# Attention with exact row maxima on one core: the maxima's matmuls move to 48-row operands in the two row halves of TensorE, in batches of four heads

## The chip, the cores and the metric

One core of a Trainium2 chip runs the whole kernel. The metric is the device time of one execution in microseconds (us). A comparison is made with runs of the kernel before on the same chip.

## What is computed

x is 2 x 2048 x 256. Sixteen heads of 16 channels attend causally, in float32, then comes an output projection, a residual with layer norm, a product of int8-quantised rows with int8-quantised weights, and a second residual with layer norm.

```python
Q, K, V = (proj(Wq), proj(Wk), proj(Wv))                 # x @ W.T, split into 16 heads of 16
scores = scale * einsum('bhtd,bhsd->bhts', Q, Kb)        # keys in the future: -inf
m_new = maximum(m, max(scores, -1)); p = exp(scores - m_new)
l = corr * l + sum(p);  acc = corr * acc + p @ Vb        # corr = exp(m - m_new)
x = layernorm(x + (acc / l) @ Wo.T)
x = layernorm(x + int8_rows(x) @ int8_columns(rhs))      # times the scales of rows and columns
```

## The kernel before

The 32 pairs of batch and head are worked in 8 groups of 4 heads (HG = 4). Queries come in 4 chunks of 512 columns (CHUNKS, CH), keys in blocks of 128. A step (STEPS) is one chunk of queries against one block of keys, for the four heads of a group; a group has 40 steps, of which the last four of each chunk lie on the diagonal and are only 512, 384, 256 and 128 columns wide.

The front (0 to 127 us) projects Q and K and splits each value into three bf16 parts, whose sum is the float32 value. The parts are stored in DRAM (qparts, kparts) and come back as stacks: QS and KS hold 96 rows, six products of parts (Q_TERMS, K_TERMS), 16 channels each. Three more rows of QS hold the row's maximum, negated and split in three, against three rows of ones in KS, so that one matmul over 99 rows gives score minus maximum.

So each score is computed twice. First the maxima: an item (ITEMS) is one tile of 128 queries against up to 512 keys for two heads. Its two matmuls (L683, 96 rows, each followed on the diagonal by a mask matmul, L686) fill one of the two slots of ps_max, two banks each, and VectorE reduces the slot to block_max (L956). A group has 80 items, 32 of them on the diagonal (8 of each width 512, 384, 256 and 128). combine folds them per chunk, a transposition (turn_maxima, L694), ScalarE (L891) and GpSimd (split_maxima, L1186 to L1193) make the three rows, and SyncE writes them into QS (load_max_rows). Then the scores: one matmul a head and step (L728) into one of the three banks of ps_score, ScalarE takes the exponential (L908), GpSimd cuts the diagonal, and two steps later the values' matmuls (L709, float32, four heads side by side in four groups of 32 columns of the array) add it to ps_acc. ScalarE copies ps_acc per chunk (copy_acc, L896), SyncE stores it (store_heads).

The order on TensorE is written out by a planner at build time: quota walks the steps with costs in columns and says after which score matmul which item comes (QUOTA). The 46 first items (AHEAD) of a group are made during the group before, those of group 0 in the front (FRONT_QUOTA). Groups 0 to 5 are of kind "steady" (80 items each), group 6 is "full" (114, since it also makes all that is left for group 7), group 7 is "last" (none; the end of the kernel, per half chunk, is woven into it). Groups 1 to 4 run in a hardware loop of two turns of two groups; the others are straight-line code.

QS and KS exist twice (p = group modulo 2): while one group is worked, SyncE's queue loads the other's (next_stacks, 12 DMAs a chunk, L407), between the stores of heads and the rows of maxima.

Of the kernel before, what the change touches and what calls it, by code (L numbers as in the profile page):

```python
# [39 lines left out]
K_TERMS = [0, 0, 0, 1, 1, 2]  # L40
MIX_FROM = 12
# [27 lines left out]
def build(nc, x, wq, wk, wv, wo, ffn, out):  # L69
# [9 lines left out]
    KROWS = STACK + PARTS  # L79
    assert (B, D, DH, HALVES) == (2, 256, 16, 2) and T % (2 * CH) == 0  # L80
# [13 lines left out]
    assert NI % MAX_SLOTS == 0  # L94
# [15 lines left out]
    FORM, LOAD, READ, READ_FROM = 576, 256, 2.5, 340  # L110

    def quota(stream):
# [3 lines left out]
        made = lambda m: PAIR * (max(ITEM_COLS[m] // PAIR, LOAD) + (P if ITEMS[m][1] == ITEMS[m][0] // TPC else 0))  # L116
        read = lambda m: READ_FROM + READ * ITEM_COLS[m]

        def place(pace, early):
            at, done, free, seen, n, out = 0, 0, [0] * MAX_SLOTS, 0, 0, []  # L120
            for k, (c, kb) in enumerate(STEPS):
                out.append([])
                for j in range(HG):
                    at += max(CH - skip(c, kb), LOAD)
                    if n < len(stream) and free[n % MAX_SLOTS] <= at + early and seen * pace <= at:
                        at = max(at, free[n % MAX_SLOTS]) + made(stream[n][1])
                        done = max(done, at) + read(stream[n][1])
                        free[n % MAX_SLOTS] = done
                        seen += read(stream[n][1])
                        n += 1  # L130
# [102 lines left out]
    with ExitStack() as ctx:  # L233
# [20 lines left out]

        QS_words = sb("QS", [P, 2 * HG * T // 2], F32)
        QS = QS_words[:, :].bitcast(BF16).rearrange("p (s c j n) -> p s c j n", s=2, c=CHUNKS, j=HG)
        KS = sb("KS", [KROWS, 2, CHUNKS, HG, CH], BF16)
# [52 lines left out]
        room = [(end_words[:, :], 6), (V_words, 8), (QS_words[:, 0:HG * T // 2], 4)]  # L310
# [52 lines left out]
        s_qs = [[sem(f"q_stack{p}_in{c}") for c in range(CHUNKS)] for p in range(2)]  # L363
        s_ks = [[sem(f"k_stack{p}_in{c}") for c in range(CHUNKS)] for p in range(2)]
# [15 lines left out]
        SL = 16 * len(Q_TERMS)  # L380
        OST = 16 * (HG + 1)
# [19 lines left out]
        with nc.Block() as block:  # L401
            @block.sync
            def _(sp):
                def load_stack(q, p, c, stack, src, terms, done):

                    for t, a in enumerate(terms):
                        sp.dma_start(stack[DH * t:DH * t + DH, p, c, :, :],  # L407
                                     src[a, bass.ds((2 * q + p) * GR, GR), c * CH:c * CH + CH]
                                     .rearrange("(j d) n -> d j n", d=DH)).then_inc(done, 16)

                def load_stacks(q, p, c):
                    load_stack(q, p, c, QS, qparts, Q_TERMS, s_qs[p][c])
                    load_stack(q, p, c, KS, kparts, K_TERMS, s_ks[p][c])

                def load_max_rows(g, p, c):
                    wait_apart(sp, s_ms, splits(g, c), sp_mark)
                    for a in range(PARTS):
                        sp.dma_start(QS[STACK + a:STACK + a + 1, p, c].rearrange("a j (r n) -> a (j r) n", r=TPC),
                                     max_parts[:, c, a, :]).then_inc(s_mrow[c], 16)
# [9 lines left out]
                def group(q, p):  # L429
                    g, kind = 2 * q + p, KIND(2 * q + p)  # L430
                    first = isinstance(g, int) and g == 0
                    nq, np_ = (q, 1) if p == 0 else (q + 1, 0)

                    def next_stacks(c):
                        if not first:
                            load_stacks(nq, np_, c)

                    if not first:
                        wait_apart(sp, s_st, score_base(g), sp_mark)
                    next_stacks(0)  # L440
# [37 lines left out]
                for n in range(XCHUNKS):  # L478
                    if n + 2 < XCHUNKS:
                        load_x(n + 2)  # L480
                    if n == FRONT_TURN + 1:
                        for c in EARLY:
                            load_max_rows(0, 0, c)
                    store_parts(n)
                    if n < CHUNKS:
                        sp.wait_ge(stored[n % 2], 16 * QK_UNITS * (n // 2 + 1))
                        load_stacks(0, 0, n)
                    else:
                        load_stacks(0, 1, n - CHUNKS)
# [9 lines left out]
                def load(m):  # L499
# [3 lines left out]
                    if m == SLOTS - 2:  # L503
                        sp.wait_ge(s_st, score_base(GROUPS - 1))
# [29 lines left out]
                with sp.Fori(0, GROUPS // 2 - 2) as h:  # L534
# [16 lines left out]
                for c in LATE:  # L551
                    load_max_rows(GROUPS - 1, 1, c)
# [21 lines left out]
            def _(pe):  # L574
# [69 lines left out]
                def front():  # L644
# [7 lines left out]
                    for n in range(XCHUNKS):  # L652
                        for u in range(UNITS_X):
# [10 lines left out]
                            for m in range(done, FRONT_QUOTA[n][u]):  # L664
# [3 lines left out]
                                item(0, 0, m)  # L668
# [4 lines left out]
                def item(q, p, n):  # L673

                    i, b, w, h = ITEMS[n]
                    if n in FIRST_ITEM:
                        pe.wait_ge(s_qs[p][i // TPC], SL * (q + 1))
                        pe.wait_ge(s_ks[p][i // TPC], SL * (q + 1))
                    at_least(pe, s_reduced, item_use(2 * q + p, n) - MAX_SLOTS + 1)
                    diag = b == i // TPC  # L680
                    for t in range(PAIR):
                        bank, j = ps_max[:, n % MAX_SLOTS * PAIR + t, :], h * PAIR + t
                        m = pe.matmul(bank[:, 0:w], QS[0:STACK, p, i // TPC, j, i % TPC * P:i % TPC * P + P],  # L683
# [608 lines left out]
```

## Time and profile before

| | |
|---|---|
| median of 3 runs | 1066.67 us (1065.55 to 1070.85) |
| the profiled execution | 1070.6 us, span 1068.8 us |
| PE busy | 1000.2 us, 94% |
| DVE busy | 828.0 us, 77% |
| ACT busy | 707.8 us, 66% |
| POOL busy | 264.4 us, 25% |
| DMA moved | 66.39 MB, 62 GB/s |

PE is TensorE's matmuls, PEld its weight loads, DVE VectorE, ACT ScalarE, POOL GpSimd, SPq SyncE's queue. A matmul's duration contains its way through the array, and consecutive ones overlap; what counts is the distance from one start to the next. The copies of ps_acc at L896 mark the stages: each group has four, at fixed steps, so the distance between the same copy of two groups is the length of a group.

### The profile page before, as it was taken

How to read it: one execution, taken by the hardware profiler on the slowest of the kernel's cores; microseconds unless marked ns; L12 is line 12 of the kernel's file. 1: busy time of each engine (PE TensorE's matmuls, PEld its weight loads, DVE VectorE, ACT ScalarE, POOL GpSimd, SP SyncE). 2: the span in 40 equal slices, each digit the busy share in tenths (PEclk: the TensorE clock that was granted, in tenths of full speed). 3: DMA queues.
4: the chain of work that ended last, by engine and by line, in shares of the span. 5: the costliest groups of instructions: out<-in, count | busy, mean ns of one | idle time of the engine just before them, and what ended most of it. 6: DMA issues, size and time to landing. Idle time of an engine off the chain costs nothing.

```text
span 1068.8 us, 20004 instructions
## 1 busy us (share of the span) xinstructions
PE 1000.2 (94%) x6280; PEld 396.8 (37%) x6280; DVE 828.0 (77%) x1083; ACT 707.8 (66%) x1471; POOL 264.4 (25%) x435
## 2 busy tenths in 40 slices
PE   8999999999999999899999999999999899998972
PEld 5555433333333333233333333333333222443431
DVE  5466677777878777678777777877888888599897
ACT  3444467777777778577777777777766466787730
POOL 3534520112111211120112011201111101565644
PEclk9999989999999999999999999999999999999995
DMA  5657500002011201120102010301120420315501
GB/s 167 188 170 229 162 10 7 7 22 81 7 38 31 72 7 37 29 61 21 37 11 80 17 37 18 85 7 36 35 72 7 115 44 1 101 50 154 152 30 50
DMA packets 71786, 66.39 MB, mean 62 GB/s; under 512 B 15112, under 2 KB 65608, under 8 KB 71684
## 3 DMA queue, kind: packets, MB, share of 16 engines
q1 hardware_dynamic: 71684, 65.10, 21.8%
q8 instruction: 56, 0.92, 0.4%
q14 instruction: 46, 0.38, 0.1%
HBM read 43.25 MB, written 21.35 MB: 60 GB/s over the span
## 4 chain that ended last, share of the span: by engine, by line
PE 82%; DVE 7%; ACT 3%; DMA 3%; issue 2%; POOL 1%; SPq 1%; ACTq 0%; POOLq 0%; DVEq 0%
PE ps_acc L709 24%; PE ps_score L728 22%; PE ps_max L683 21%; PE ps_score L602 5%; DVE block_max L956 4%; PE ps_score L609 3%; ACT PR L908 2%; PE ps_max L686 2%; PE ps_max L783 1%; DMA end_slots<-heads_out 1%; PE ps_acc L583 1%; DMA V<-heads_out 1%; DMA row_sums<-accS 1%; ACT accS L896 1%; PE ps_score L694 1%
## 5 line engine op out<-in xcount | busy, mean ns | idle before, releaser
L956 DVE TENSOR_REDUCE block_max<-ps_max 128x2 f32<-128x1024 f32 (+3 forms) x640 | 658.1, 1062 | 191.5 <-PE ps_max L683 95.0
L908 ACT ACTIVATE PR<-ps_score 128x512 f32<-128x512 f32 (+3 forms) x1280 | 618.9, 536 | 225.3 <-PE ps_score L728 210.0
L728 PE MATMUL ps_score<-QS,KS 99*128 99x512 bf16 (+3 forms) x1280 | 392.9, 354 | 20.2 <-ACT PR L908 12.7
L683 PE MATMUL ps_max<-KS,QS 96*128 96x512 bf16 (+3 forms) x1280 | 359.3, 351 | 15.2 <-DVE block_max L956 12.1
L709 PE MATMUL ps_acc<-PR,VG 128*32 128x512 f32 (+3 forms) x2560 | 303.3, 546 | 0.1
L728 PEld LDWEIGHTS ps_score<-QS,KS 99*128 99x128 bf16 x1280 | 118.9, 97 | 339.3 <-ACT PR L908 233.4
L683 PEld LDWEIGHTS ps_max<-KS,QS 96*128 96x128 bf16 x1280 | 120.5, 98 | 106.3 <-DVE block_max L956 42.0
L1178 POOL TENSOR_SCALAR_AFFINE_SELECT PR<-PR 128x512 f32<-128x512 f32 x128 | 81.7, 638 | 314.7 <-ACT PR L908 314.5
L686 PE MATMUL ps_max<-mask_q,ident_b 128*128 128x128 bf16 x512 | 102.6, 220 | 0.0
L709 PEld LDWEIGHTS ps_acc<-PR,VG 128*32 128x32 f32 x2560 | 50.7, 108 | 96.6 <-ACT PR L908 54.9
L1186 POOL CAST max_parts<-neg_max 16x128 bf16<-16x128 f32 (+1 forms) x31 | 8.8, 285 | 275.7 <-ACT neg_max L891 272.5
L602 PE MATMUL ps_score<-PR,wT 128*128 128x512 f32 x128 | 60.4, 598 | 0.8 <-ACT neg_max L870 0.7
L686 PEld LDWEIGHTS ps_max<-mask_q,ident_b 128*128 128x128 bf16 x512 | 50.6, 99 | 22.7 <-issue 2.8
L1165 POOL TENSOR_TENSOR end_slots<-PR,end_slots 128x512 bf16<-128x512 f32 x32 | 37.0, 1157 | 65.0 <-ACT end_slots L857 65.0
L852 ACT CAST end_slots<-ps_score 128x512 bf16<-128x512 f32 x32 | 18.8, 586 | 45.8 <-PE ps_score L602 45.8
L602 PEld LDWEIGHTS ps_score<-PR,wT 128*128 128x128 f32 x128 | 23.5, 192 | 21.0 <-issue 18.2
L609 PE MATMUL ps_score<-wT,PR 128*128 128x256 f32 x128 | 31.3, 391 | 0.0
L1170 POOL COPY VG<-V 128x256 f32<-128x256 f32 (+1 forms) x32 | 12.6, 394 | 71.7 <-PE ps_acc L709 71.3
L1005 DVE TENSOR_TENSOR PR<-ps_score,end_slots 128x512 f32<-128x512 f32 x32 | 21.8, 684 | 8.0 <-ACT end_slots L852 7.0
L609 PEld LDWEIGHTS ps_score<-wT,PR 128*128 128x128 f32 x128 | 24.4, 194 | 4.4
L896 ACT COPY accS<-ps_acc 128x512 f32<-128x512 f32 x32 | 19.1, 597 | 7.7 <-PE ps_acc L709 7.6
L1221 POOL TENSOR_TENSOR rstd<-var_eps,minus_half 128x2 f32<-128x2 f32 x32 | 23.5, 734 | 2.7
(122 smaller groups left out, 465.3 us busy)
## 6 DMA issues: line engine op xcount, KB each, us to landing
QS<-qparts SPq DMA_DIRECT2D x192, 64.0 KB, 2.3
KS<-kparts SPq DMA_DIRECT2D x192, 64.0 KB, 2.3
qparts<-end_slots SPq DMA_DIRECT2D x16, 384.0 KB, 5.3
kparts<-end_slots SPq DMA_DIRECT2D x16, 384.0 KB, 4.5
PR<-in_L_attn_x SPq DMA_DIRECT2D x8, 512.0 KB, 4.4
heads_out<-accS SPq DMA_DIRECT2D x124, 32.0 KB
end_slots<-in_L_attn_x SPq DMA_DIRECT2D x4, 512.0 KB, 9.8
out_y<-end_slots SPq DMA_DIRECT2D x8, 256.0 KB, 2.1
```

The source lines that it names most:

```text
L602: m = pe.matmul(bank, wT[:, w, mh, nh * P:nh * P + P], xT[:, n % 2, mh, :], start=mh == 0, stop=mh == HALVES - 1)
L609: m = pe.matmul(bank[:, t * D:t * D + D], xT[:, n % 2, mh, tile * P:tile * P + P], wT[:, 2, mh, :], start=mh == 0, stop=mh == HALVES - 1)
L683: m = pe.matmul(bank[:, 0:w], QS[0:STACK, p, i // TPC, j, i % TPC * P:i % TPC * P + P], KS[0:STACK, p, b, j, 0:w], start=True, stop=not diag)
L686: m = pe.matmul(bank[:, w - P:w], ident_b[:, :], mask_q[:, :], start=False, stop=True)
L709: m = pe.matmul(ps_acc[EYE * j:EYE * j + EYE, s:CH], VG[:, kb, j, :], PR[:, k % 4, j, 0:CH - s], start=kb == 0, stop=k == LAST[c])
L728: pe.matmul(bank[:, 0:CH - s], KS[:, p, kb // TPC, j, kb % TPC * P:kb % TPC * P + P], QS[0:KROWS, p, c, j, s:CH], start=True, stop=True).t ...
L896: act.copy(accS[:, c % 2, :], ps_acc[:, :]).then_inc(s_accS, 1)
L908: act.activation(PR[:, k % 4, j, 0:w], ps_score[:, score_slot(pos), 0:w], ACT.Exp, scale=SCALE).then_inc(s_exp, 1)
L956: dve.tensor_reduce(block_max[:, h * PAIR:h * PAIR + PAIR, i, b], ps_max[:, slot_at:slot_at + PAIR, 0:w], AX.X, ALU.max).then_inc(s_reduce ...
L1165: pool.tensor_tensor(parts[:, n % 2, u, 2, :], rest[:, q % RESTS, :], parts[:, n % 2, u, 1, :], ALU.subtract).then_inc(part3, 1)
L1178: pool.affine_select(out=block, in_=block, compare_op=ALU.is_ge, fill=0.0, base=0, pattern=[[0, HG], [1, P]], channel_multiplier=-1).then_ ...
L1221: pool.tensor_tensor(rstd[:, z, which, rows], var_eps[:, z, which, rows], minus_half[:, :], ALU.pow)\
```

## The change

1. Maxima's operands. New tensors QM and KM hold 48 rows (MROWS: three products of parts, MAX_TERMS) for a head in rows 0 to 47 and for a second head in rows 64 to 111 (ROW_HALF), two halves a group, two groups. They replace the 96-row stacks for the maxima (the maximum is thus computed from fewer parts; scores minus maxima still use all six products). The two matmuls of an item now read the two row halves and write two banks.
2. Items come in batches of two (four heads). On the diagonal the mask matmuls of the whole batch come first, and wait until both slots are free; the 48-row matmuls are then added on top. The planner prices a pair as one matmul and a batch with SEEN = 480 columns more.
3. QS and KS exist once. A chunk of QS is loaded for the next group when this group's last step of that chunk has been scored, a chunk of KS when the last chunk of queries has passed it. The operands of maxima for the next group are loaded at the group's start, 12 DMAs of 128 KB.
4. The loop over groups 1 to 4 is written out on every engine.
5. The ones of KS are set in 4 memsets, not 8; the end's buffers lie in QM and KM.

In the front, items are still made one by one.

```diff
+MAX_TERMS = [(0, 0), (1, 0), (0, 1)]
+ROW_HALF = 64
-    FORM, LOAD, READ, READ_FROM = 576, 256, 2.5, 340
+    FORM, LOAD, READ, READ_FROM, SEEN = 576, 256, 2.5, 340, 480
-        made = lambda m: PAIR * (max(ITEM_COLS[m] // PAIR, LOAD) + (P if ITEMS[m][1] == ITEMS[m][0] // TPC else 0))
+        made = lambda m: max(ITEM_COLS[m] // PAIR, LOAD) + (PAIR * P if ITEMS[m][1] == ITEMS[m][0] // TPC else 0)
+        later = lambda m: SEEN + made(m) if ITEMS[m][1] < ITEMS[m][0] // TPC else 0
...
-                    if n < len(stream) and free[n % MAX_SLOTS] <= at + early and seen * pace <= at:
-                        at = max(at, free[n % MAX_SLOTS]) + made(stream[n][1])
-                        done = max(done, at) + read(stream[n][1])
+                    if n < len(stream) and seen * pace <= at and max(free[0], free[1] - later(stream[n][1])) <= at + early:
+                        at += SEEN
+                        for m in stream[n:n + MAX_SLOTS]:
+                            at = max(at, free[n % MAX_SLOTS]) + made(m[1])
+                            done = max(done, at + SEEN) + read(m[1])
...
+                def load_max_operands(g, p, done, t0=0, t1=T):
+                    for r in range(PAIR):
+                        for t, (a, b) in enumerate(MAX_TERMS):
+                            at = ROW_HALF * r + DH * t
+                            for rows, src in ((QM[at:at + DH, p, :, t0:t1], qparts[a]), (KM[at:at + DH, p, :, t0:t1], kparts[b])):
+                                sp.dma_start(rows, src[bass.ds(g * GR, GR), t0:t1]
+                                             .rearrange("(h r d) t -> r d h t", r=PAIR, d=DH)[r]).then_inc(done, 16)
...
                     if not first:
                         store_heads(g - 1, CHUNKS - 1)
-                    load_max_rows(g, p, 2)
+                    load_max_rows(g, 2)
+                    if not first:
+                        wait_apart(sp, s_reduced, NI * g, sp_mark)
+                        load_max_operands(g + 1, 1 - p, s_am[1 - p])
+                    next_q(0)
                     store_heads(g, 0)
-                    next_stacks(1)
-                    next_stacks(2)
+                    next_q(1)
                     store_heads(g, 1)
-                    load_max_rows(g, p, 3)
-                    load_max_rows(g + 1, np_, 0)
+                    load_max_rows(g, 3)
+                    load_max_rows(g + 1, 0)
...
-                    next_stacks(3)
+                    next_q(2)
                     store_heads(g, 2)
-                    load_max_rows(g + 1, np_, 1)
+                    next_k(0)
+                    load_max_rows(g + 1, 1)
+                    for c in range(1, CHUNKS):
+                        next_k(c)
+                    next_q(3)
...
+                def items(q, p, some):
+                    for n in some:
+                        i, b, w, h = ITEMS[n]
+                        if b == i // TPC:
+                            at_least(pe, s_reduced, item_use(2 * q + p, n) - MAX_SLOTS + 1)
+                            for t in range(PAIR):
+                                pe.matmul(ps_max[:, n % MAX_SLOTS * PAIR + t, w - P:w], ident_b[:, :], mask_q[:, :],
+                                          start=True, stop=True)
+                    for n in some:
...
+                        if b != i // TPC:
+                            at_least(pe, s_reduced, item_use(2 * q + p, n) - MAX_SLOTS + 1)
+                        for t in range(PAIR):
+                            r = ROW_HALF * t
+                            m = pe.matmul(ps_max[:, n % MAX_SLOTS * PAIR + t, 0:w], QM[r:r + MROWS, p, h, i * P:i * P + P],
+                                          KM[r:r + MROWS, p, h, b * CH:b * CH + w], start=b != i // TPC, stop=True,
+                                          skip_group_check=b == i // TPC)
+                        m.then_inc(s_piece, 1)
...
-                pe.wait_ge(s_set, 1 + 2 * CHUNKS)
+                pe.wait_ge(s_set, 1 + CHUNKS)
...
-                with pe.Fori(0, GROUPS // 2 - 2) as h:
+                for h in range(GROUPS // 2 - 2):
                     group(h, 1)
                     group(h + 1, 0)
```

## Rows read from the trace of the kernel before

**Rows 1.** The page: the chain that ended last, shares of the span by engine.

```profile
PE 82%; DVE 7%; ACT 3%; DMA 3%; issue 2%; POOL 1%; SPq 1%; ACTq 0%; POOLq 0%; DVEq 0%
```

**Rows 2.** Busy time by stretch: start:end, length, PE, PEld, DVE, ACT, POOL, clock.

```profile
555.00:660.00 105.00, 104.07 (x710) 37.52 (x708) 82.46 (x85) 79.27 (x168) 16.88 (x36) 1.00 0.13 37
```

**Rows 3.** Timeline, last copy of ps_acc of groups 0, 1, 2, 4, 5, 6: start, duration (us).

```profile
240.14 0.59 ACT L896 COPY accS<-ps_acc 128x512 f32<-128x512 f32 x1
...
345.67 0.59 ACT L896 COPY accS<-ps_acc 128x512 f32<-128x512 f32 x1
...
457.67 0.59 ACT L896 COPY accS<-ps_acc 128x512 f32<-128x512 f32 x1
...
668.75 0.59 ACT L896 COPY accS<-ps_acc 128x512 f32<-128x512 f32 x1
...
773.68 0.59 ACT L896 COPY accS<-ps_acc 128x512 f32<-128x512 f32 x1
...
910.27 0.66 ACT L896 COPY accS<-ps_acc 128x512 f32<-128x512 f32 x1
```

**Rows 4.** Timeline of one steady step: values, score, item, three scores, item, values.

```profile
600.65 0.39 PE L728 MATMUL ps_score<-QS,KS 99*128 99x512 bf16 x1
600.66 0.32 PEld L683 LDWEIGHTS ps_max<-KS,QS 96*128 96x128 bf16 x2
600.87 0.60 PE L683 MATMUL ps_max<-KS,QS 96*128 96x512 bf16 x2
601.31 0.89 PE L728 MATMUL ps_score<-QS,KS 99*128 99x512 bf16 x3
601.51 2.38 DVE L956 TENSOR_REDUCE block_max<-ps_max 128x2 f32<-128x1024 f32 x2 [0.53 <-PE ps_max L683]
602.03 0.60 PE L683 MATMUL ps_max<-KS,QS 96*128 96x512 bf16 x2
602.56 1.06 PE L709 MATMUL ps_acc<-PR,VG 128*32 128x512 f32 x8
603.55 0.10 PEld L728 LDWEIGHTS ps_score<-QS,KS 99*128 99x128 bf16 x1 [0.84 <-ACT PR L908]
```

**Rows 5.** Timeline, values' matmuls of 128 columns between two scores.

```profile
239.44 0.43 PE L709 MATMUL ps_acc<-PR,VG 128*32 128x128 f32 x8
239.79 0.80 PE L728 MATMUL ps_score<-QS,KS 99*128 99x256 bf16 x3
```

**Rows 6.** Groups by shape: busy us, mean ns.

```profile
L956 DVE TENSOR_REDUCE block_max<-ps_max 128x2 f32<-128x768 f32 x64 | 59.9, 957 | 28.9 <-PE ps_max L686 28.3
L956 DVE TENSOR_REDUCE block_max<-ps_max 128x2 f32<-128x512 f32 x64 | 42.6, 688 | 12.2 <-PE ps_max L686 11.9
L956 DVE TENSOR_REDUCE block_max<-ps_max 128x2 f32<-128x256 f32 x64 | 26.3, 423 | 22.4 <-PE ps_max L686 22.0
```

**Rows 7.** Timeline where the loop turns back: TensorE's first instruction, SyncE's DMAs.

```profile
450.14 0.61 PE L728 MATMUL ps_score<-QS,KS 99*128 99x512 bf16 x1 [3.40 <-issue]
450.18 3.73 SPq L407 DMA_DIRECT2D KS<-kparts  x6
```

**Rows 8.** Timeline in group 6: VectorE, and an item that waits for it.

```profile
861.12 3.49 DVE L956 TENSOR_REDUCE block_max<-ps_max 128x2 f32<-128x1024 f32 x3 [0.46 <-PE ps_max L683]
862.40 0.61 PE L683 MATMUL ps_max<-KS,QS 96*128 96x512 bf16 x2 [0.45 <-DVE block_max L956]
```

**Rows 9.** Timeline of the front and of its end.

```profile
108.66 0.60 PE L683 MATMUL ps_max<-KS,QS 96*128 96x512 bf16 x2
109.10 1.89 PE L609 MATMUL ps_score<-wT,PR 128*128 128x256 f32 x8
...
125.21 0.59 ACT L864 COPY V<-ps_score 128x512 f32<-128x512 f32 x1 [1.06 <-PE ps_score L609]
127.30 0.39 PE L728 MATMUL ps_score<-QS,KS 99*128 99x512 bf16 x1 [1.69 <-POOL KS L1258]
131.69 1.89 PE L728 MATMUL ps_score<-QS,KS 99*128 99x384 bf16 x5
```

More of the change, by code:

```diff
@@ L667, in front @@
                                     pe.wait_ge(f_copied, 2)
-                                item(0, 0, m)
+                                items(0, 0, [m])
                             done = FRONT_QUOTA[n][u]
@@ L671, in front @@
                             turn_first_maxima()
[L673 to L683, printed above, removed]
-                                      KS[0:STACK, p, b, j, 0:w], start=True, stop=not diag)
-                        if diag:
-                            m = pe.matmul(bank[:, w - P:w], ident_b[:, :], mask_q[:, :], start=False, stop=True)
-                    m.then_inc(s_piece, 1)
+                def items(q, p, some):
[7 more added lines that the diff above has]
+                    for n in some:
+                        i, b, w, h = ITEMS[n]
+                        if n in FIRST_ITEM and isinstance(q, int) and (q, p) == (0, 0):
+                            pe.wait_ge(s_first[i // TPC], AM)
+                        elif n == 0:
+                            pe.wait_ge(s_am[p], AM * (q + p))
+                        if b != i // TPC:
[6 more added lines that the diff above has]
+                        m.then_inc(s_piece, 1)
@@ L727, in group @@
                             bank = ps_score[:, score_slot(pos), :]
-                            pe.matmul(bank[:, 0:CH - s], KS[:, p, kb // TPC, j, kb % TPC * P:kb % TPC * P + P],
-                                      QS[0:KROWS, p, c, j, s:CH], start=True, stop=True).then_inc(s_st, 1)
-                            while n < QUOTA[kind][k][j]:
-                                on, m = STREAM[kind][n]
-                                item(*groups[on], m)
-                                n += 1
+                            pe.matmul(bank[:, 0:CH - s], KS[:, kb // TPC, j, kb % TPC * P:kb % TPC * P + P],
+                                      QS[:, c, j, s:CH], start=True, stop=True).then_inc(s_st, 1)
+                            if n < QUOTA[kind][k][j]:
+                                on = STREAM[kind][n][0]
+                                some = [m for o, m in STREAM[kind][n:QUOTA[kind][k][j]] if o == on]
+                                items(*groups[on], some)
+                                n += len(some)
                             if kind == "last" and j % 2:
@@ L821, in _ @@
                 group(0, 0)
-                with pe.Fori(0, GROUPS // 2 - 2) as h:
+                for h in range(GROUPS // 2 - 2):
                     group(h, 1)
@@ L934, in _ @@
                 group(0, 0)
-                with act.Fori(0, GROUPS // 2 - 2) as h:
+                for h in range(GROUPS // 2 - 2):
                     group(h, 1)
@@ L1061, in _ @@
                 group(0, 0)
-                with dve.Fori(0, GROUPS // 2 - 2) as h:
+                for h in range(GROUPS // 2 - 2):
                     group(h, 1)
@@ L1263, in _ @@
                 group(0, 0)
-                with pool.Fori(0, GROUPS // 2 - 2) as h:
+                for h in range(GROUPS // 2 - 2):
                     group(h, 1)
```

74 lines of the change are left out of this document (39 added, 35 removed).

## The prediction, made before the changed kernel ran

> **What bounds the kernel now.** I read the page's chain of waits first [rows 1]: the chain that ended last is 82% TensorE. Then the stages: the last copy of ps_acc of each group [rows 3] gives 105.53 us for group 1 (345.67 - 240.14), 112.00 for group 2 (457.67 - 345.67), twice 105.54 for groups 3 and 4 (668.75 - 457.67) and 104.93 for group 5. Group 6, which reads 114 items, takes 910.27 - 773.68 = 136.6. The busy time by stretch comes next: in a steady group of 105 us [rows 2] TensorE is busy 104, VectorE 82, ScalarE 79, GpSimd 17: TensorE is the bound there, with VectorE 20% behind. The timeline of one step [rows 4] says what the 105 us are made of: a matmul of 512 columns starts 0.22 us after the one before it (two of an item take 0.44), and its weights are loaded while the one before it streams, so a load costs nothing. In group 6 it is VectorE: three reads without a gap in 3.49 us, and an item that waits 0.45 us for them [rows 8].
>
> **Part 1, the pairs (gain).** Two heads in two row halves should stream in the time of one. Of the 80 items of a group 56 are 512 wide, and 8 each 384, 256 and 128. A pair saves 0.22 us at 512 [rows 4] and, in proportion to the columns, 0.165 and 0.11; at 128 I take nothing. 56 x 0.22 + 8 x 0.165 + 8 x 0.11 = 14.5 us a group. No row shows row halves at work. The nearest is the values: four heads in four column groups, float32, 8 instructions of 512 columns, done in 1.00 us [rows 4]; with 128 columns in 0.35 [rows 5]. That is 0.65 us for 384 columns more, 1.7 ns a column for all four heads, four cycles at 2.4 GHz: the four heads run at once at full rate. So I take full overlap; the lower bound is none (rival C).
>
> **Part 2, going into the halves and out (cost).** The same rows show what it costs to change how the array is cut. The last item before the values starts at 602.03 and streams until 602.47; the values start at 602.56, 0.09 later. Their slope puts 512 columns at 0.86 us, and the next score's weights start 0.99 us and the score 1.00 us after them, so 0.14 to come back; at 128 columns 0.35 - 0.22 = 0.13. The score's weights are loaded only at 603.55, when the values are through: on this border a load isn't hidden. Together 0.25 us there and back, taking the entry as 0.10. I call the same cost for a batch X. Its bounds: 0 (the row cut needs no emptying of the array, as between two matmuls of equal cut) and 0.35 (going in loads weights of 128 columns, not of 32, for two halves; a recorded load is 0.10 us, unhidden). I take 0.25, the row nearest to it. Worked through by its own rule, the planner places every item of a steady group in pairs: 40 batches, 10.0 us a group.
>
> The Trainium skill, page "TensorEngine Tiling (Array Packing)", section "Key Properties", says that changing the tiling mode drains TensorE, which speaks against this change; the gaps around the values agree with it, and no row shows whether it holds for rows as for columns. By that sentence X isn't 0. The page "TensorE: Matmul & The Clock Gate", Part 3, has weight loads overlap running matmuls only in another row group; the second pair of a batch would then pay its load, 0.10 us more. The load under a running matmul of the same rows [rows 4] speaks against it for the whole array, and none shows it for the halves.
>
> **Part 3, waiting for both slots.** Before, an item needs one free slot while VectorE reads the other, which hides TensorE's work. A batch off the diagonal keeps this: its first pair goes into slot 0 while slot 1 is read. A batch on the diagonal (16 of 40) starts its masks only when both are free. VectorE starts 0.42 us after the second matmul of an item starts (601.51 against 601.09), and a batch of two full items keeps it 2.38 us [rows 4]. So a batch that begins at b has both slots free at about b + 0.1 + 0.42 + 2.38 = b + 2.9. The next comes a step later: 4 scores 0.88, batch 0.44 + 0.25, values with their border 1.10 = 2.67. On the diagonal it waits 0.25 us if it directly follows a full batch, less or nothing if the plan put it later, as it often does. 16 x 0.15 = 2.5 us a group; bounds 0 and 16 x 0.35 = 5.6. Behind the waiting instruction in TensorE's queue stand the scores, for which ScalarE waits: it has some 25 us of slack a group [rows 2].
>
> A steady group: -14.5 + 10.0 + 2.5 = -2.0 us. Six of them (0 to 5): -12.
>
> **Part 4, group 6.** VectorE bounds it. Its 114 reads are 84 of 1.19 us [rows 4] and 10 each of 0.96, 0.69 and 0.42 [rows 6]: 121 us, the group 136.6. Halving TensorE's work there frees nothing. New is that VectorE idles in each of 21 diagonal batches from the end of its last read to the first pair: 4 masks of 128 columns 0.22, entry 0.1, 0.42 until it may read, with the masks' wait together 0.8 us, or 16 us; and the plan puts its last batch at step 35, with some 5.5 us of scores behind it. 121 + 16 + 5.5 = 142.5, +6 us. Bounds: 0 (its idle time in group 6 before is as long, and may be replaced) and +12 (0.15 us at each other batch too).
>
> **Part 5, the front.** Items are still single there, and TensorE is back to back: an item of 512 takes 0.44 us between two projections [rows 9]. 46 borders at 0.25 = 11.5 us, against 28 full items x 0.22 + 6 x 0.165 + 6 x 0.11 = 7.8 saved: +3.7.
>
> **Part 6, the start of group 0.** TensorE waits 1.69 us for the memset of ones, while the copy it needs too ended at 125.80 [rows 9]. With four memsets fewer it starts some 1.4 us earlier. After that gap five scores of 384 take 1.89 us [rows 9], half speed: the clock fell to 1.2 GHz. If it doesn't, up to 5 us more; I take 2. Sum -3.4 (0 to -6.4).
>
> **Part 7, the loop.** Where it turns back, TensorE waits 3.40 us for nothing the profile shows [rows 7] and then runs at half clock for a while; group 2 is 6.4 us longer than group 1 [rows 3]. There is one such turn. Straight-line groups (5, 6) show no such stop, so the longer program should cost nothing: -6.4 (0 if a fetch of instructions takes its place).
>
> **Part 8, SyncE's queue and single stacks: nothing.** Stacks still cost 48 DMAs a group, plus 12 of the new operands; six issue in 3.7 us [rows 7], so 7.5 us more of some 50. The tightest new wait is K's chunk 0: released at step 27, needed 13 steps later, some 34 us, against 4 us of issue and the landing. Behind it stand the next group's rows of maxima for chunk 1, which are turned only at step 31. Q's and K's chunk 3 come at step 39 and are needed at step 24 of the next group. If one did come late, TensorE would stop at the head of a chunk; none has less than 10 us in hand.
>
> **The sum,** against the profiled execution's 1070.6 us: -12 + 6 + 3.7 - 3.4 - 6.4 = -12.1, or 1058.5. Written with X open: 987 + 286 X. The median of the runs shown is 3.9 us under the profiled one, so 1054.6; I say **1054 us**, 1.2% faster.
>
> **The rivals.**
> A, the border of the halves is cheap, X from 0 to 0.2. For it: only column cuts are seen to cost. At 0.15 the sum gives 1030, as a median 1026.
> B, slower: the border costs more than the values' one, since each way in must load 128 columns of weights unhidden for both halves. X = 0.35: 1087, as a median 1083. It decides from X = 0.29, where the sum equals the time before; the place is each of the 286 batches. For it: the score's load at 603.55 waits for the values' end. Against: 0.14 us for the way back already has such a load in it. The rule on loads named above is this rival by another mechanism: +0.10 a batch, the same 0.35.
> C, the halves don't run at once: no pair saves. 987 + 94.8 + 71.5 = 1153, as a median 1149. Against it the values' four heads at once.
> D, VectorE becomes the bound in steady groups. Its 82 us plus 16 x 0.8 plus 24 x 0.27 (the second batch's read begins 0.25 us after the first's end) is 101; with every misplaced batch added, groups stay at 105, and the sum is 1070.6 + 6 + 3.7 - 9.8 = 1070.5, as a median 1067.
>
> **Chances.** Forecast 0.45, A 0.22, B 0.16, D 0.12, C 0.05. Low end: A down to X = 0.13, 1020. High end: B at 1084. What lies outside is C and the tails of A and B, some 2 in 10. Half a per cent, 1061 to 1072, is about what a measurement here can tell: faster 0.60 (A and most of the forecast), same 0.16 (D and the edge of the forecast), slower 0.24 (B, C, the upper edge).
>
> **What would show it.** The distance between equal copies of ps_acc: 103.5 us in groups 1 to 5 with none at 112, 142 in group 6. In a full step the distance from the score before a batch to the score after it: 0.22 + 0.69. The two matmuls of a pair start within 0.1 us of each other and the next pair 0.22 later; if 0.44, C. VectorE's gap before a diagonal batch 0.8 us. No TensorE wait on a DMA. The prediction is wrong first of all through X, at 2.9 us for each 0.01 of it.

## The result, and the profile after

The changed kernel takes 1072.9 us (median of 20 runs, 1067.0 to 1079.0), the kernel before in the same runs 1065.9. The ratio is 1.0061, 95% interval 1.0043 to 1.0079: slower by 0.6%, where 1054 and 1.2% faster were forecast. The time lies inside the stated range (1020 to 1084), on the other side of no change.

The page of the changed kernel, in the rows that moved: busy time and share, the slices, the chain.

```profile
PE 968.6 (90%) x6280; PEld 325.9 (30%) x6280; DVE 816.7 (76%) x1083; ACT 693.2 (65%) x1471; POOL 256.7 (24%) x431
PE   8999999999999999999999999999887888998862
PEclk9999999999999999999999999999999789999995
PE 63%; DVE 23%; ACT 7%; DMA 3%; issue 2%; SPq 1%; POOL 1%; POOLq 0%; DVEq 0%; ACTq 0%
```

TensorE is busy 32 us less than before, and the span is 1.6 us longer. In the chain that ended last VectorE has gone from 7% to 23% and ScalarE from 3% to 7% [rows 1]: TensorE now waits for others. The slices of group 6 (the 29th to the 34th) have lost their nines, and two of them (0.7 and 0.8) show a lower granted clock.

The last copy of ps_acc of groups 0, 1, 2, 5 and 6 in the changed kernel, as in [rows 3]:

```profile
236.09 0.58 ACT L931 COPY accS<-ps_acc 128x512 f32<-128x512 f32 x1
...
341.04 0.58 ACT L931 COPY accS<-ps_acc 128x512 f32<-128x512 f32 x1
...
445.99 0.58 ACT L931 COPY accS<-ps_acc 128x512 f32<-128x512 f32 x1
...
761.37 0.61 ACT L931 COPY accS<-ps_acc 128x512 f32<-128x512 f32 x1
...
911.53 0.66 ACT L931 COPY accS<-ps_acc 128x512 f32<-128x512 f32 x1
```

Distances between such copies, here and for the experiments below (us; the end of group 0 is the copy's own time). The distances are those of one profiled execution each, the medians those of 20 runs (changed), 4 to 10 (e1, e2, e5, e7, e9, e10), 2 (e3, e4, e8) or 1 (e6, e11):

| kernel | end of 0 | a steady group | group 6 | median |
|---|---|---|---|---|
| before | 240.1 | 105.5, one of 112.0 | 136.6 | 1065.9 |
| changed | 236.1 | 104.95 | 150.2 | 1072.9 |
| e1, before, loop written out | 233.5 | 104.7 | 137.4 | 1058.8 |
| e2, diagonal batches in turn | 236.3 | 105.5 | 133.6 | 1058.2 |
| e3, reads halved | 230.2 | 100.2 | 119.0 | 1010.3 |
| e4, exponentials halved | 233.1 | 102.3 | 149.5 | 1053.4 |
| e5, in turn in group 6 only | 237.0 | 104.95 | 134.1 | 1056.4 |
| e6, e3 and e4 together | 227.0 | 97.4 | 115.7 | 989.3 |
| e7, batch in mid step | 237.5 | 105.4, two longer | 135.2 | 1061.0 |
| e8, single items | 236.5 | 104.6 | 131.2 | 1051.7 |
| e9, the same again | 234.6 | 104.6 | 132.4 | 1051.0 |
| e10, single items at two places | 234.7 | 102.3 | 133.0 | 1039.2 |
| e11, both heads in one half | 256.4 | 118.3 | 155.6 | 1163.8 |

So groups 1, 3 and 4 gained 0.6 us each at first sight (group 5, at 105.5, lost as much), the turn of the loop is gone, and group 6 gave 13.6 us back. One step of a steady group, TensorE alone, is the counterpart of [rows 4]:

```profile
628.23 0.38 PE L762 MATMUL ps_score<-QS,KS 99*128 99x512 bf16 x1
628.54 0.61 PE L718 MATMUL ps_max<-KM,QM 48*128 48x512 bf16 x4
629.08 0.82 PE L762 MATMUL ps_score<-QS,KS 99*128 99x512 bf16 x3
629.83 1.06 PE L743 MATMUL ps_acc<-PR,VG 128*32 128x512 f32 x8
630.83 0.61 PE L762 MATMUL ps_score<-QS,KS 99*128 99x512 bf16 x2
```

The batch of four matmuls takes 0.54 us from its start to the next score: 2 x 0.216 for two pairs, 0.11 to come out. It starts 0.31 after the score, 0.22 of streaming and 0.10 to go in. So the halves do run at once, and a border costs 0.21 us (in and out together), not 0.25. That much of the mechanism works: this step takes 2.60 us, where one of before takes 2.91 (603.56 - 600.65, the second from the score at 603.56 that follows the row at 603.55 in [rows 4]). The gain is lost elsewhere. Here is the start of a diagonal batch in group 6:

```profile
802.52 0.38 PE L762 MATMUL ps_score<-QS,KS 99*128 99x512 bf16 x1
802.52 0.32 PEld L706 LDWEIGHTS ps_max<-mask_q,ident_b 128*128 128x128 bf16 x2
802.74 0.28 PE L706 MATMUL ps_max<-mask_q,ident_b 128*128 128x128 bf16 x2
...
803.34 0.28 PE L706 MATMUL ps_max<-mask_q,ident_b 128*128 128x128 bf16 x2 [0.33 <-DVE block_max L991]
803.56 0.61 PE L718 MATMUL ps_max<-KM,QM 48*128 48x512 bf16 x4
803.99 2.36 DVE L991 TENSOR_REDUCE block_max<-ps_max 128x2 f32<-128x1024 f32 x2 [0.71 <-PE ps_max L718]
```

TensorE sets the masks of the first slot, stands until VectorE has freed the second, and VectorE then stands 0.71 us until the first pair is there. Both engines idle in turn.

### The profile page after: what moved, and what is told of

It reads as the page before. It is cut to its first block, busy times and chain, and to the rows that moved or that the text cites. A ratio compares the mean times of both kernels' runs of the same rounds, so it can differ in the third digit from the quotient of the medians.

```text
span 1070.4 us, 17302 instructions
## 1 busy us (share of the span) xinstructions
PE 968.6 (90%) x6280; PEld 325.9 (30%) x6280; DVE 816.7 (76%) x1083; ACT 693.2 (65%) x1471; POOL 256.7 (24%) x431
## 4 chain that ended last, share of the span: by engine, by line
PE 63%; DVE 23%; ACT 7%; DMA 3%; issue 2%; SPq 1%; POOL 1%; POOLq 0%; DVEq 0%; ACTq 0%
DVE block_max L991 19%; PE ps_acc L743 19%; PE ps_score L762 18%; PE ps_max L718 12%; ACT PR L943 6%; PE ps_score L628 5%; PE ps_max L706 3%; PE ps_score L635 2%; PE ps_max L818 2%; DMA end_slots<-heads_out 1%; ACT accS L931 1%; PE ps_acc L609 1%; DMA kparts<-end_slots 1%; DVE stats L1105 1%; DMA row_sums<-accS 1%
## 5 line engine op out<-in xcount | busy, mean ns | idle before, releaser
L991 DVE TENSOR_REDUCE block_max<-ps_max 128x2 f32<-128x1024 f32 (+3 forms) x640 | 649.2, 1061 | 194.5 <-PE ps_max L718 192.8
L943 ACT ACTIVATE PR<-ps_score 128x512 f32<-128x512 f32 (+3 forms) x1280 | 604.9, 537 | 253.2 <-PE ps_score L762 250.4
L762 PE MATMUL ps_score<-QS,KS 99*128 99x512 bf16 (+3 forms) x1280 | 361.7, 356 | 28.4 <-ACT PR L943 24.5
L718 PE MATMUL ps_max<-KM,QM 48*128 48x512 bf16 (+3 forms) x1280 | 198.3, 357 | 29.3 <-DVE block_max L991 22.9
L762 PEld LDWEIGHTS ps_score<-QS,KS 99*128 99x128 bf16 x1280 | 97.7, 97 | 380.8 <-ACT PR L943 289.3
L718 PEld LDWEIGHTS ps_max<-KM,QM 48*128 48x128 bf16 x1280 | 49.1, 94 | 133.3 <-DVE block_max L991 86.4
L706 PE MATMUL ps_max<-mask_q,ident_b 128*128 128x128 bf16 x512 | 56.7, 223 | 8.5 <-DVE block_max L991 7.9
L706 PEld LDWEIGHTS ps_max<-mask_q,ident_b 128*128 128x128 bf16 x512 | 40.5, 99 | 34.0 <-DVE block_max L991 13.3
L1205 POOL COPY VG<-V 128x256 f32<-128x256 f32 x32 | 12.7, 396 | 158.1 <-PE ps_acc L743 157.9
```

What stands on the lines that cost most here:

```text
L706: pe.matmul(ps_max[:, n % MAX_SLOTS * PAIR + t, w - P:w], ident_b[:, :], mask_q[:, :], start=True, stop=True)
L718: m = pe.matmul(ps_max[:, n % MAX_SLOTS * PAIR + t, 0:w], QM[r:r + MROWS, p, h, i * P:i * P + P], KM[r:r + MROWS, p, h, b * CH:b * CH + w] ...
L762: pe.matmul(bank[:, 0:CH - s], KS[:, kb // TPC, j, kb % TPC * P:kb % TPC * P + P], QS[:, c, j, s:CH], start=True, stop=True).then_inc(s_st, 1)
L943: act.activation(PR[:, k % 4, j, 0:w], ps_score[:, score_slot(pos), 0:w], ACT.Exp, scale=SCALE).then_inc(s_exp, 1)
L991: dve.tensor_reduce(block_max[:, h * PAIR:h * PAIR + PAIR, i, b], ps_max[:, slot_at:slot_at + PAIR, 0:w], AX.X, ALU.max).then_inc(s_reduce ...
```

## The experiments

Two theories were set against each other first. Theory 1: the loss is in slots, above all the wait for both before a diagonal batch. Theory 2: four heads in one batch keep ScalarE and the score banks waiting.

**e1.** The kernel before, with the loop alone written out:

```diff
-                with pe.Fori(0, GROUPS // 2 - 2) as h:
+                for h in range(GROUPS // 2 - 2):
```

> The kernel before with nothing changed but the loop over groups 1 to 4 written out on all five engines. If the 3.4 us stop of TensorE and the half clock behind it belong to the loop's turn back, group 2 falls from 112.0 to 105.5 us and the kernel is 6.4 us faster (ratio 0.994). Rival: the fetch of a longer program takes the stop's place somewhere else, and the ratio is 1.000. If the former holds, the pairs and batches by themselves cost about 13 us against this kernel, where the changed kernel's whole loss is 7.

Measured: 1058.8 us, ratio 0.9921 (0.9893 to 0.9949). The expectation holds and is too small. The stop of 3.4 us is gone (group 2: 112.0 to 104.7), and the other three groups of the loop are 0.8 us shorter each (105.5 to 104.7), down to what straight-line group 5 always took (104.9, rows of 668.75 and 773.68 in [rows 3]). By the copies 9.7 us of groups 1 to 5 come from the loop. Against this kernel the pairs and batches are not 7 us slower but 14: steady groups 104.95 against 104.72, group 6 150.2 against 137.4. This is the fair base for all that follows.

**e2.** A diagonal batch item by item:

```diff
-        later = lambda m: SEEN + made(m) if ITEMS[m][1] < ITEMS[m][0] // TPC else 0
+        later = lambda m: SEEN + made(m)
...
-                        at += SEEN
                         for m in stream[n:n + MAX_SLOTS]:
+                            at += SEEN if n % MAX_SLOTS == 0 or ITEMS[m[1]][1] == ITEMS[m[1]][0] // TPC else 0
...
                     for n in some:
                         i, b, w, h = ITEMS[n]
+                        at_least(pe, s_reduced, item_use(2 * q + p, n) - MAX_SLOTS + 1)
                         if b == i // TPC:
-                            at_least(pe, s_reduced, item_use(2 * q + p, n) - MAX_SLOTS + 1)
...
-                    for n in some:
-                        i, b, w, h = ITEMS[n]
...
-                        if b != i // TPC:
-                            at_least(pe, s_reduced, item_use(2 * q + p, n) - MAX_SLOTS + 1)
```

The first lines change the planner's prices, so the plan changes too: in a steady group 34 of the 40 batches stand behind another score than before, and in group 6 the last batch comes later.

> The changed kernel, but a batch on the diagonal is made item by item: wait for slot 0, its masks, its pair, then wait for slot 1, its masks, its pair; the planner is told so. It goes in and out of the row halves twice, 0.21 us more in each of 16 (group 6: 21) batches, and no longer needs both slots free. Theory 1 (the wait for both slots before a diagonal batch leaves VectorE idle, which costs group 6 its 13.6 us and the steady groups most of their gain): group 6 from 150.2 to about 138, steady groups from 105.0 to 103 or less, the kernel to about 1050. Theory 2 (four heads in one batch keep ScalarE and the score banks waiting, and the slots hardly matter): steady groups 105 plus 16 x 0.21 = 108, group 6 150 or more, the kernel some 20 us slower than the changed one.

Measured: 1058.2 us, 0.9923 (0.9896 to 0.9950). Group 6 falls from 150.2 to 133.6, as theory 1 has it and further than it said. Where the diagonal batches paused VectorE, it now reads ten items in a row without a gap:

```profile
784.51 11.16 DVE L987 TENSOR_REDUCE block_max<-ps_max 128x2 f32<-128x1024 f32 x10 [0.35 <-PE ps_max L714]
788.74 0.28 PE L706 MATMUL ps_max<-mask_q,ident_b 128*128 128x128 bf16 x2
788.95 0.34 PE L714 MATMUL ps_max<-KM,QM 48*128 48x384 bf16 x2
789.26 0.28 PE L706 MATMUL ps_max<-mask_q,ident_b 128*128 128x128 bf16 x2
789.48 0.34 PE L714 MATMUL ps_max<-KM,QM 48*128 48x384 bf16 x2
```

In the whole of group 6 VectorE's waits for TensorE fall from 22.2 to 13.7 us. But the new plan is worth as much. The last read of group 6 ends 11.6 us before the copy that closes the group in the changed kernel, 4.8 before it in the kernel before, and 3.0 before it here (copies at 911.53, 910.27 and 897.73). The last reads of the three, in this order:

```profile
897.59 2.36 DVE L991 TENSOR_REDUCE block_max<-ps_max 128x2 f32<-128x1024 f32 x2 [1.52 <-PE ps_max L718]
...
903.11 2.36 DVE L956 TENSOR_REDUCE block_max<-ps_max 128x2 f32<-128x1024 f32 x2 [0.20 <-PE ps_max L686]
...
892.40 2.36 DVE L987 TENSOR_REDUCE block_max<-ps_max 128x2 f32<-128x1024 f32 x2 [0.17 <-PE ps_max L714]
```

So of the 16.6 us about half are waits of VectorE (8.5) and about half the time behind its last read (8.6). No run takes the one without the other.

Steady groups come to 105.5: 0.6 more, where 16 further borders cost 16 x 0.21 = 3.4. So some 2.8 us of waits are gone there, and neither theory's figure (103; 108) was met. Which waits they were, e3 shows.

**e3, e4.** One engine relieved at a time:

```diff
-                    dve.tensor_reduce(..., ps_max[:, slot_at:slot_at + PAIR, 0:w],
+                    dve.tensor_reduce(..., ps_max[:, slot_at:slot_at + PAIR, 0:w // 2],
...
-                            act.activation(PR[:, k % 4, j, 0:w], ps_score[:, score_slot(pos), 0:w], ACT.Exp,
+                            act.activation(PR[:, k % 4, j, 0:w // 2], ps_score[:, score_slot(pos), 0:w // 2], ACT.Exp,
```

> The changed kernel with each of VectorE's reads of the maxima's banks over the first half of the columns only (the second half is left out of the maxima): 0.69 us in place of 1.22 at full width. The plan stays. Theory 1 (TensorE loses its time to slots that VectorE hasn't freed): steady groups from 105.0 to about 98, group 6 from 150 to about 112. Theory 2 (ScalarE): steady groups stay at 103 or more; group 6 falls to about 125, since there the reads are the bound by either theory.

> The changed kernel with ScalarE's exponential over the first half of the columns only (the rest is left out of the values' sums): about 0.39 us in place of 0.60. Theory 2 (TensorE waits for score banks because scores now come in bunches): steady groups from 105.0 to 99 or less. Theory 1: steady groups stay within 1.5 us of 105, group 6 within 2 us of 150.

Measured: 104.95 falls to 100.2 with halved reads and to 102.3 with halved exponentials. Both theories hold in part, and neither alone. Group 6 falls to 119.0 with the reads (112 was expected) and stays at 149.5 with the exponentials: there theory 1 stands alone.

These two kernels have the same matmuls in the same order as the changed one, 708 between two such copies of a steady group, so the distances from start to start can be set side by side. With halved reads 17 of them are shorter. Fourteen are the start of the second pair of a batch off the diagonal (3.6 us together), two the first pair of such a batch (0.3), and only one is a mask (0.65). With halved exponentials 13 starts of scores are shorter, 2.7 us together. One of the fourteen, in the changed kernel:

```profile
497.66 1.22 DVE L991 TENSOR_REDUCE block_max<-ps_max 128x2 f32<-128x1024 f32 x1
498.27 0.39 PE L718 MATMUL ps_max<-KM,QM 48*128 48x512 bf16 x2
498.94 0.39 PE L718 MATMUL ps_max<-KM,QM 48*128 48x512 bf16 x2 [0.27 <-DVE block_max L991]
499.26 0.29 PE L762 MATMUL ps_score<-QS,KS 99*128 99x128 bf16 x2
```

and the same place in e3:

```profile
481.80 0.61 PE L718 MATMUL ps_max<-KM,QM 48*128 48x512 bf16 x4
482.34 0.29 PE L762 MATMUL ps_score<-QS,KS 99*128 99x128 bf16 x2
```

The first pair goes out, the second stands until VectorE has left its slot at 498.88: 0.67 us after the first, where 0.22 would do. So in steady groups the wait of the diagonal masks for both slots is 0.65 us in one batch of 16, and the slots cost most where the batch was thought to be safe. That the in-turn form still saved 2.8 us fits VectorE getting the first of two diagonal items earlier and coming to the batches behind it with less in arrears, or the moved batches; the two weren't told apart.

**e5.** The in-turn form in group 6 only (the call of items gets `kind == "full"`, and so does the plan's price).

> The changed kernel with the diagonal batches made item by item in group 6 alone (steady groups keep their batches, where making them in turn gave 105.5 us against 105.0). If the two effects are independent: steady groups 104.95, group 6 at 133.6, the kernel 3.5 us under the version with all of them in turn, about 1055, faster than both kernels.

Measured: 1056.4 us, 0.9913 (0.9883 to 0.9942); 104.95 and 134.1. The two effects are independent, as expected. It beats the kernel before by 0.9%, but its interval overlaps almost all of that of e1: with the batches mended, the pairs are just paid back.

**e6.** The edits of e3 and e4 together.

> The changed kernel with both the reads and the exponentials over half the columns. Halved reads took 4.75 us from a steady group, halved exponentials 2.6. If the two are separate waits of TensorE, together 7.4: 97.6 us, which is what TensorE's own work comes to (104.7 us with single items, less 14.5 for the pairs, plus 40 x 0.21 for the borders, less some 0.7 of waits). If they are one and the same wait, the group stays near 100.

Measured: 97.4 us a steady group, in a single run (97.6 by the sum, 97.6 by adding the two savings). The waits are separate. TensorE's own work in the changed kernel is thus at most 97.4, since 0.7 us of waits for ScalarE are left in this trace. The account of a steady group: 97.4 of work and these, 4.75 of waits for slots (0.65 of it for both at once), 2.6 of waits for ScalarE, 104.8 of 104.95.

**e7.** Built on e5: in steady groups batches come only after the second or third score.

```diff
-                    if n < len(stream) and seen * pace <= at and ...
+                    if n < len(stream) and (full or j in (1, 2)) and seen * pace <= at and ...
```

> As the version with group 6 in turn, but in steady groups a batch may follow only the second or the third score matmul of a step, not the first or last (the planner places them anew). If TensorE's wait for ScalarE comes from three scores in a bunch behind a batch that directly follows the first score, steady groups fall from 104.95 to about 103. If it comes from the total of ScalarE's work or from the narrow steps, no change within 0.5 us; if the planner pays for it with waits for slots, 106 or more.

Measured: 1061.0 us, 0.9950 (0.9925 to 0.9975), 4.6 us over e5; steady groups 105.4, two of them 106.7 and 108.1 (granted clock 0.98 and 0.97). No gain, and the trace says why: TensorE's idle time before scores falls, from 2.6 us a steady group in the changed kernel to 1.5, and that before maxima's matmuls rises, from 2.3 to 2.8. Besides, the five batches that stood directly before the values, with one border only (see e8), are gone. So the place of a batch does bear on the waits for ScalarE, and what it gives is paid back.

**e8, e9.** The row halves without batches, at the places of the plan of before:

```diff
-                            if n < QUOTA[kind][k][j]:
-                                on = STREAM[kind][n][0]
-                                some = [m for o, m in STREAM[kind][n:QUOTA[kind][k][j]] if o == on]
-                                items(*groups[on], some)
-                                n += len(some)
+                            while n < QUOTA[kind][k][j]:
+                                on, m = STREAM[kind][n]
+                                items(*groups[on], [m])
+                                n += 1
```

> The row halves without batches: every item by itself, at the places that the plan of the kernel before gives it, loop written out. No item waits for more than its own slot; there are 80 borders in a steady group, not 40. With 0.21 us each: 104.7 - 14.5 + 16.8 = 107.0 us a steady group, group 6 at 137 (VectorE bounds it), the kernel about 1072. If the border is dearer for a single item (0.28 us, as the front's look), 112.

> The kernel with single items once more, for an interval: it came out at 1051.7 us where 1072 was expected. Theory now: a border costs 0.10 us in and 0.11 out; an item that stands directly before the values pays only one of the two, and no item waits for two slots, so a steady group is again TensorE's own work (104.6 us), and group 6 gains 6 us, since each item there takes TensorE 0.2 us less. Ratio to the kernel before 0.986, clear of 0.9921 for the kernel before with its loop written out. If the first look was luck with the clock, 0.992.

Measured: 1051.7, then 1051.0 us, 0.9865 (0.9829 to 0.9900), an interval that still touches that of e1 (from 0.9893). The first expectation was 20 us off. Steady groups take 104.6, not 107.0, as long as in e1 (104.7): single pairs save in the steady groups what their borders cost. Group 6 takes 131.2 and 132.4, not 137 (granted clock 1.00 and 0.99), and that is the gain over e1. The trace of e8 shows one reason why the borders cost less than 80 x 0.21: an item between the last score and the values.

```profile
595.03 0.28 PE L703 MATMUL ps_max<-mask_q,ident_b 128*128 128x128 bf16 x2
595.24 0.28 PE L715 MATMUL ps_max<-KM,QM 48*128 48x256 bf16 x2
595.45 1.06 PE L740 MATMUL ps_acc<-PR,VG 128*32 128x512 f32 x8
```

256 columns stream in 0.11 us; the values start 0.10 after that, which is what they cost behind a score anyway (0.09 in [rows 4]). From row halves to column groups there is one border, not two. Nine of the 80 items stand so, which is some 1 us of the 2.4 missed. By e11 below, which has the same borders and no overlap, all 80 cost 118.3 - 104.7 = 13.6 us, 0.17 each; the rest of the difference isn't explained, waits that the borders took the place of among it. TensorE is busy again for all of the group:

```profile
547.00:652.00 105.00, 104.25 (x714) 30.99 (x714) 83.27 (x85) 81.00 (x169) 17.05 (x36) 1.00 0.28 52
```

**e10.** That observation as a plan: in steady groups an item may follow only the second or the fourth score.

```diff
-                    if n < len(stream) and free[n % MAX_SLOTS] <= at + early and seen * pace <= at:
-                        at = max(at, free[n % MAX_SLOTS]) + made(stream[n][1])
+                    if n < len(stream) and (len(stream) > NI or j % 2) and free[n % MAX_SLOTS] <= at + early and ...:
+                        at = max(at, free[n % MAX_SLOTS]) + border(j) + made(stream[n][1])
```

made counts a pair once here, and border is 250 columns after the fourth score, 500 elsewhere.

> Single items, but in steady groups only behind the second and the fourth score matmul of a step: 40 of 80 items stand directly before the values in place of 9. If such an item saves 0.10 us of border, 31 x 0.10 = 3.1 us: steady groups from 104.6 to 101.5, the kernel 15 to 18 us faster than with items at the old places. If the border there is the same, or if two items at fixed places wait for VectorE, steady groups 104 or more.

Measured: 1039.2 us, 0.9737 (0.9702 to 0.9772), the fastest of those that compute everything, 2.6% under the kernel before and 1.9% under e1. A step of it, from its trace:

```profile
621.41 0.61 PE L760 MATMUL ps_score<-QS,KS 99*128 99x512 bf16 x2
621.95 0.39 PE L716 MATMUL ps_max<-KM,QM 48*128 48x512 bf16 x2
622.27 0.61 PE L760 MATMUL ps_score<-QS,KS 99*128 99x512 bf16 x2
622.81 0.39 PE L716 MATMUL ps_max<-KM,QM 48*128 48x512 bf16 x2
623.13 1.06 PE L741 MATMUL ps_acc<-PR,VG 128*32 128x512 f32 x8
624.13 0.61 PE L760 MATMUL ps_score<-QS,KS 99*128 99x512 bf16 x2
```

Two items in 2.72 us: the second pair starts 0.32 before the values, 0.216 of streaming and 0.10 of border. A steady group is 102.3, 2.4 us less than with items at the old places (3.1 expected). Groups 1 to 5 give 11.6 us of the 11.5 between the spans of e9 and e10; group 0, a steady one too, ends at the same time in both, since its first 17 us ran at a granted clock of 0.80 in e10 and of 1.00 in e9. That, and 2.4 us a group in place of 3.1, is why the 15 us expected weren't reached.

**e11.** Both matmuls of an item in rows 0 to 47, single items (`r = 0` in place of `ROW_HALF * t`).

> Single items at the old places, but both matmuls of an item read rows 0 to 47 (so the second head's maxima are those of the first). Two matmuls of one row half can't stream at once: if the overlap of the halves is all that the pair saves, a steady group is 14.5 us longer than with the halves, 119, and the second matmul starts 0.22 us behind the first; if the gain came from the shorter operands, 105.

Measured: 118.3 us a steady group, 13.7 more than with the halves (a single run). In its trace a pair of 512 takes 0.54 us to the next score, where the halves take 0.32:

```profile
621.29 0.39 PE L759 MATMUL ps_score<-QS,KS 99*128 99x512 bf16 x1
621.61 0.60 PE L715 MATMUL ps_max<-KM,QM 48*128 48x512 bf16 x2
622.15 0.39 PE L759 MATMUL ps_score<-QS,KS 99*128 99x512 bf16 x1
```

So all that the pair saves is the overlap, and it saves what Part 1 of the prediction worked out.

## Why the prediction was wrong, step by step

The changed kernel was to be 12.1 us under the profiled execution of before; its own profile has a span 1.6 us longer. By the copies of ps_acc the 13.6 us between the two are 8.1 in groups 1 to 5 (8.3 gained, 16.4 forecast), 7.6 in group 6, 0.3 behind it, less 2.4 in the front and group 0.

- **Part 1, pairs, -14.5 a group: right.** e11 puts it at 13.7.
- **Part 2, the border, 0.25 us: nearly right.** 0.21, taken from the column groups' border, is 8.4 us a group and not 10. The Trainium skill, page "TensorEngine Tiling (Array Packing)", section "Key Properties", says that a change of tiling mode drains TensorE, and for rows the trace agrees: 0.10 us in, 0.11 out. The Trainium skill, page "TensorE: Matmul & The Clock Gate", Part 3, lets a weight load overlap running matmuls only in another row group; that would show as 0.10 more between the two pairs of a batch. They start 0.22 us apart (four matmuls and the way out in 0.54), so the trace doesn't agree.
- **Part 3, waiting for slots, +2.5 a group: the step that failed.** It put the wait at the masks of diagonal batches, and said of the others that they keep the overlap of before, and of ScalarE that it has 25 us of slack. e3 and e4 show the reverse. The masks wait 0.65 us a group, in one batch of 16. The batches off the diagonal wait 3.9 us, since the second pair follows the first at 0.22 us and finds VectorE still in its slot, and TensorE waits 2.6 us for ScalarE. That is 7.4 us a group in place of 2.5. e1 with single 96-row items takes 104.7 us, e6 with batches 97.4: with some 7 us of work gone, TensorE came within reach of the others. Slack of an engine over a whole group is no cover for three scores in a row within 0.65 us; e7, which moves the batches, takes part of that wait away. The steady group was to gain 2.0; with X right it would have been 3.6; against e1 it lost 0.2.
- **The base.** I took 105.5 us as the length of a steady group and the loop's cost as its one turn. The loop costs each of its groups 0.8 us as well; so even the 0.6 us that a steady group seems to gain comes from the loop, not from the pairs. The group of before outside the loop stood in [rows 3] with 104.93, and I didn't ask why it was shorter.
- **Part 4, group 6, +6, bounded at +12: too small.** It is +12.7 against e1, +13.6 against before. VectorE's busy time is as before, 115.9 against 117.2 us. Its waits for TensorE grew from 13.5 us to 22.2, and the time behind its last read from 4.8 to 11.6. The gap before a diagonal batch is real: at full clock it is 0.60 us on average (16 batches, most of them 0.55 to 0.71), where 0.8 was forecast. Four more lie in or right behind stretches at 1.2 GHz, 1.5 to 3.1 us each, and the forecast had no term for the clock. TensorE's idle time before the maxima's matmuls grew from 11.6 to 22 us, and the granted clock of group 6 is 0.91, before 0.99 and in e1 0.98. That e5 and e2 take 16.1 and 16.6 us away, against the 16 of the forecast, is luck in part: half of it is the later last batch of their plan. What the clock cost wasn't separated by a run. An estimate comes from the 20 runs of the changed kernel: 1078.4 us at a granted clock of 0.960 over the whole run, 1067.0 at 0.984, 4.7 us for each 0.01 by a straight line through all. Their median clock is 0.970, that of e1's runs 0.980, so some 5 of the 14 us between the two would be the clock's.

```profile
761.37:911.53 150.16, 126.65 (x785) 33.77 (x784) 115.86 (x124) 79.76 (x169) 17.80 (x37) 0.91 0.28 58
```

- **Part 5, the front, +3.7: too large.** From the start of the first item to that of the last it takes 89.5 us (36.03 to 125.54) in the changed kernel and 87.5 (34.93 to 122.40) in e1: +2.0, and 1.1 of it is one wait for the operands KM, which I had not named. In the profiled execution of before it takes 89.5 too, with the granted clock at 0.91 from 40 to 60 us, which is why the front seems to cost nothing there.
- **Part 6, the start, -3.4: half shown.** TensorE's wait for the memset, 1.69 us, is down to 0.50: -1.2, near the 1.4 forecast.

```profile
126.43 0.38 PE L762 MATMUL ps_score<-QS,KS 99*128 99x512 bf16 x1 [0.50 <-issue]
```

The half clock behind it [rows 9] doesn't come back, but it isn't there in e1 either, which keeps the same 1.69 us; and e7 and e10, which have the shorter wait, run at a granted clock of 0.50 from 132.8 and 131.9 us on. So it belongs to the execution and not to the memset, and I should have charged nothing for it.
- **Part 7, the loop, -6.4: right in kind, too small.** 9.7 by e1.
- **Part 8, single stacks and SyncE's queue, nothing: right.** From the start of group 0 on TensorE waits for no stack and no operand, though the kernel moves 78.8 MB, not 66.4.
- **The rivals.** D came nearest: VectorE in the chain and no gain in steady groups. Its price was right for them (105) and too low for group 6. But its mechanism holds in part only: VectorE is busy 82 of the 105 us, and ScalarE's share of the waits was not in it. It compared VectorE's sum, 101 us, with TensorE's; both sums lay below 105, and the group still took that, since the engines wait for each other in turn. B and C are out by the trace, A by 0.01 us.

## What to carry to other kernels

When work is taken from the bounding engine, ask what it will wait for at each hand-over, not only which sum is next: TensorE with 97 us of work and VectorE with 82, two slots between them, took 105, with 4.8 of it at the slots and 2.6 at ScalarE's banks. A batch that fills all buffers in a row undoes double buffering, even where it waits for them one by one: here its second half waited more often than its first. One buffer at a time, with a plan to match, gave 16 us back in one group. And a change of the array's cut is paid per border, so put work of one odd cut next to work of another odd cut: 31 fewer half borders were worth 2.4 us a group.

## What the runs showed of the hardware

- Two bf16 matmuls in rows 0 to 47 and 64 to 111 stream at once at full rate: 0.22 us for both at 512 columns (e10), 0.43 in one half (e11).
- Going from the whole array to row halves costs 0.10 us and back 0.11. Going from row halves to groups of 32 columns costs 0.10, as much as from the whole array, so one of two borders vanishes.
- The hardware loop here costs more than its turn: 0.8 us in each group of some 105 (e1), on top of 3.4 us of stop and the half clock behind it at the turn.
